# All four queues written in another order between the output projection and the third normalisation of a decoder layer

## The reference

```python
x = x + attn(_layernorm(x), Wqkv, bqkv, Wo, bo)            # one head, 256 wide
x = x + xattn(_layernorm(x), ctx_4096, scales, zero_points)
x = x + ffn(_layernorm(x), c1_w, c2_w, w1, w2t)

def xattn(x1, x2, ...):
    fake_quant(x, s, z) = (clip(round(x / s + z), 0, 255) - z) * s
    return matmul(fake_quant(x1), fake_quant(x2))           # (512x1024) @ (1024x1024) per batch

def ffn(xf, c1_w, c2_w, w1, w2t):
    inter = xf @ c1_w.T @ c2_w.T                            # rank 16, 3584 wide
    idx = argmax of every block of 64 in inter              # one of 64 hidden units is kept
    h = relu(sum(w1[idx] * xf)); return h @ w2t[idx]
```

## Time and profile before

| | before |
|---|---|
| median of 3 runs | 806.68 us (805.74 to 808.58) |
| the profiled execution | 806.61 us, of which 804.8 us are the span of the trace |
| busy: PE, DVE, POOL, ACT | 787.0, 591.8, 432.8, 248.8 us |
| mean granted clock of TensorE | 0.997 of full speed |

### The profile page before, as it was taken

One profiled execution on the slowest core, in us unless ns is written; L12 is line 12 of the kernel. 1 busy time (PEld: TensorE's weight loads), 2 busy tenths in 40 slices (PEclk: granted clock), 3 DMA queues, 4 the chain that ended last, 5 costly groups with the idle time before them and its releaser, 6 DMA issues.

```text
span 804.8 us, 11466 instructions
## 1 busy us (share of the span) xinstructions
PE 787.0 (98%) x3884; PEld 640.1 (80%) x3888; DVE 591.8 (74%) x958; ACT 248.8 (31%) x372; POOL 432.8 (54%) x264
## 2 busy tenths in 40 slices
PE   8999998799999999999999999999999999999998
PEld 7888886358888888888888888888888888888886
DVE  6646648768786778777787878787878777787864
ACT  6456655775141121222212030303121212212030
POOL 3936797556999974352525344444444452525340
PEclk9999999999999999999999999999999999999999
DMA  9126403000101111111111110111111111111104
GB/s 344 56 105 208 157 1 109 0 8 7 40 24 50 59 53 60 53 59 52 59 52 59 52 47 19 49 54 52 59 52 59 52 59 52 59 52 52 52 11 198
DMA packets 22615, 53.22 MB, mean 66 GB/s; under 512 B 4544, under 2 KB 6592, under 8 KB 22464
## 3 DMA queue, kind: packets, MB, share of 16 engines
q1 hardware_dynamic: 22448, 51.86, 18.7%
q10 hardware_dynamic: 144, 1.05, 0.4%
HBM read 48.70 MB, written 4.19 MB: 66 GB/s over the span
## 4 chain that ended last, share of the span: by engine, by line
PE 89%; DVE 6%; ACT 3%; POOL 1%; DMA 1%; issue 1%; DVEq 0%; ACTq 0%
PE bank L1747 13%; PE bank L1748 13%; PE bank L1749 13%; PE bank L1652 12%; PE bank L1654 11%; PE bank L1653 11%; PE bank L1463 3%; PE bank L1465 3%; PE bank L1464 3%; PE bank L1661 2%; PE bank L1643 2%; PE bank L1606 1%; DVE xn L1127 1%; PE bank L1622 1%; DVE stats L1012 1%
## 5 line engine op out<-in xcount | busy, mean ns | idle before, releaser
L1747 PE MATMUL bank<-w_hi,h_hi 128*128 128x512 f32 x448 | 176.2, 393 | 0.0
L1748 PE MATMUL bank<-w_lo,h_hi 128*128 128x512 f32 x448 | 175.0, 391 | 0.0
L1749 PE MATMUL bank<-w_hi,h_lo 128*128 128x512 f32 x448 | 174.4, 389 | 0.0
L1249 DVE TENSOR_TENSOR x<-bank,x 128x512 f32<-128x512 f32 x208 | 133.4, 685 | 50.0 <-PE bank L1749 50.0
L559 POOL TENSOR_TENSOR lo_r<-r,slot 128x512 fp32r<-128x512 f32 x52 | 67.5, 1299 | 163.7 <-ACT slot L777 163.7
L1749 PEld LDWEIGHTS bank<-w_hi,h_lo 128*128 128x128 f32 x448 | 84.1, 188 | 18.0
L1747 PEld LDWEIGHTS bank<-w_hi,h_hi 128*128 128x128 f32 x448 | 84.1, 188 | 15.7
L1748 PEld LDWEIGHTS bank<-w_lo,h_hi 128*128 128x128 f32 x448 | 84.4, 188 | 15.2
L1652 PE MATMUL bank<-xT_hi,slot 128*128 128x512 f32 x240 | 95.0, 396 | 0.0
L1653 PE MATMUL bank<-xT_lo,slot 128*128 128x512 f32 x240 | 93.6, 390 | 0.0
L1654 PE MATMUL bank<-xT_hi,lo_r 128*128 128x512 f32 x192 | 74.8, 390 | 0.0
(11 more groups left out here) (203 smaller groups left out, 1598.3 us busy)
## 6 DMA issues: line engine op xcount, KB each, us to landing
r<-w SPq DMA_DIRECT2D x56, 256.0 KB, 3.4
w_raw<-w SPq DMA_DIRECT2D x28, 512.0 KB, 4.0
x<-x_in SPq DMA_DIRECT2D x8, 512.0 KB, 9.7
ctx_raw<-ctx_in SPq DMA_DIRECT2D x8, 512.0 KB, 3.9
xn<-ctx_in SPq DMA_DIRECT2D x8, 512.0 KB, 4.8
out<-x SPq DMA_DIRECT2D x7, 512.0 KB, 2.7
W_raw<-wqkv SPq DMA_DIRECT2D x6, 512.0 KB, 9.8
c_raw<-c SPq DMA_DIRECT2D x112, 16.0 KB, 2.0
```

The costliest lines, as they stand in the source:

```text
L1249: nc.vector.tensor_tensor(x[:, t, c], bank[unit_banks(g)[p]][:, :], x[:, t, c], ALU.add).then_inc(unit_added, 1)
L1747: nc.tensor.matmul(dst, h_hi[:, j, m], w2_hi[:, j, c], start=j == 0, stop=False)
L1748: nc.tensor.matmul(dst, h_hi[:, j, m], w2_lo[:, j, c], start=False, stop=False)
L1749: last = nc.tensor.matmul(dst, h_lo[:, j, m], w2_hi[:, j, c], start=False, stop=j == GJ - 1)
```

## The change

The same instructions are issued but for two PE placements that were "halfway" inside a product; their order in the queues of PE, DVE, ACT and POOL is another, and the job list with it. SP's queue is unchanged. In the order of PE: all four Wo products of the first batch come first, then the first column sums, then both O halves with nothing between them and Wo 4. Quantised products 0 and 1 stand between Wo products 5, 6 and 7. Third-norm transposes are spread between the quantised products, and those of tiles 6 and 7 come behind C11.

```diff
@@ job_order
-    jobs += both("WO", 0) + both("WO", 1) + both("WO", 2) + both("O", 1) + both("WO", 3) + both("CB", 0)
-    jobs += both("WO", 4) + both("WO", 5) + both("CB", 1) + both("WO", 6) + both("WO", 7)
...
+    for t in range(4):
+        jobs += both("WO", t)
+    jobs += both("CB", 0) + both("O", 1) + both("WO", 4) + both("WO", 5) + both("XA", 0) + both("WO", 6) + both("WO", 7)
+    jobs += both("XA", 1) + both("CB", 1) + both("XA", 2) + both("XA", 3) + both("XA", 4) + both("XA", 5)
+    jobs += both("T3", 0) + both("T3", 1) + both("XA", 6) + both("T3", 2) + both("T3", 3) + both("XA", 7)
+    jobs += both("T3", 4) + both("T3", 5)
     jobs += [("U", 0)] + both("T3", 6) + both("T3", 7)
@@ gpsimd
-            for t in range(6):
+            add_corr(0)
+            add_corr(1)
+            add_corr(2)
+            plain_lo(0, 0)
+            for t in range(3, NT):
+                add_corr(t)
...
+            for t in range(4):
                 norm3(t)
-            plain_lo(0, 0)
             plain_lo(0, 1)
-            norm3(6)
-            norm3(7)
+            for t in range(4, NT):
+                norm3(t)
@@ scalar
             variance(2, 3)
             roots(2, 0)
-            copy_q1T(7)
             variance(2, 4)
+            centre_q1(6)
+            centre_q1(7)
+            copy_q1T(6)
+            both(hi_T, 2, 0)
+            both(hi_T, 2, 1)
...
+            plain_hi(0, 2)
+            plain_hi(0, 3)
             both(hi_T, 2, 6)
             both(hi_T, 2, 7)
-            plain_hi(0, 2)
-            plain_hi(0, 3)
             hi_w2(0, 0)
@@ vector
+            for t in range(TB):
+                add_WO(t)
             copy_CB(0)
             norm_scale(1, 0)
+            lo_O(1, 0)
+            round_q1(0)
+            lo_O(1, 1)
+            round_q1(1)
             add_WO(4)
...
+            add_XA(3)
+            add_XA(4)
+            norm_scale(2, 0)
+            round_q1(6)
+            round_q1(7)
+            add_XA(5)
             row_biases()
...
             lo_u(0)
             cut_c2(0)
+            dve.wait_ge(order_ready, 1)
+            pick_first(0, 0)
             lo_T(2, 6)
             lo_T(2, 7)
@@ tensor
+            for t in range(TB):
+                project_out(t)
+            column_sums(0)
             mix_values(1, 0)
             mix_values(1, 1)
-            project_out(3)
-            column_sums(0)
             project_out(4)
-            project_out(5)
-            column_sums(1)
-            project_out(6)
             pe.wait_ge(id_b_ready, 1)
             transpose_q1(0)
+            project_out(5)
+            transpose_q1(1)
+            quantised_product(0)
+            project_out(6)
+            transpose_q1(2)
             project_out(7)
-            transpose_q1(1)
-            for t in range(6):
-                quantised_product(t, lambda: transpose_q1(t + 2))
-            quantised_product(6)
+            quantised_product(1)
+            transpose_q1(3)
+            column_sums(1)
+            quantised_product(2)
+            transpose_q1(4)
+            quantised_product(3)
+            transpose_q1(5)
+            quantised_product(4)
+            quantised_product(5)
+            transpose_q1(6)
             transpose_norm(2, 0)
             transpose_norm(2, 1)
+            quantised_product(6)
+            transpose_q1(7)
+            transpose_norm(2, 2)
+            transpose_norm(2, 3)
             quantised_product(7)
-            for t in range(2, 6):
-                transpose_norm(2, t)
+            transpose_norm(2, 4)
+            transpose_norm(2, 5)
             rank_projection(0)
-            transpose_norm(2, 6)
-            transpose_norm(2, 7)
...
             plain_hidden(0, 0, 0, within({4: [(score_pair, 0)]}))
+            transpose_norm(2, 6)
+            transpose_norm(2, 7)
             plain_hidden(0, 1, 0, within({1: [(score_pair, 1)]}))
```

More of the change, by code:

```diff
@@ L549, in norm3 @@
                                         ALU.add).then_inc(normed3, 1)
[L551 to L554, removed]
             def lo_A(g, i, raw, hi, lo):
@@ L894, in _ @@
             nc.scalar.activation(eps_root, eps, ACT.Sqrt)
-            variance(1, 0)
-            variance(1, 1)
-            variance(1, 2)
+            for t in range(TB):
+                variance(1, t)
+            roots(1, 0)
             hi_O(1, 0)
+            norm(1, 0)
             hi_O(1, 1)
-            variance(1, 3)
-            roots(1, 0)
-            norm(1, 0)
             norm(1, 1)
             centre_q1(0)
+            centre_q1(1)
             norm(1, 2)
-            centre_q1(1)
             copy_q1T(0)
             norm(1, 3)
+            plain_hi(0, 0)
             centre_q1(2)
+            centre_q1(3)
             copy_q1T(1)
-            centre_q1(3)
             roots(1, 4)
             copy_q1T(2)
+            variance(2, 0)
             norm(1, 4)
@@ L918, in _ @@
             copy_q1T(3)
+            centre_q1(5)
+            variance(2, 1)
+            copy_q1T(4)
             roots(1, 6)
-            centre_q1(5)
+            variance(2, 2)
             norm(1, 6)
-            variance(2, 0)
-            copy_q1T(4)
+            copy_q1T(5)
             norm(1, 7)
[L925 to L930, removed]
             variance(2, 3)
             roots(2, 0)
-            copy_q1T(7)
             variance(2, 4)
+            centre_q1(6)
[3 more added lines that the diff above has]
+            both(hi_T, 2, 1)
             variance(2, 5)
             roots(2, 4)
-            both(hi_T, 2, 0)
-            both(hi_T, 2, 1)
-            plain_hi(0, 0)
             plain_hi(0, 1)
-            variance(2, 6)
+            copy_q1T(7)
             both(hi_T, 2, 2)
             both(hi_T, 2, 3)
+            variance(2, 6)
+            both(hi_T, 2, 4)
+            both(hi_T, 2, 5)
             variance(2, 7)
             roots(2, 6)
-            both(hi_T, 2, 4)
-            both(hi_T, 2, 5)
             hi_u(0)
+            plain_hi(0, 2)
+            plain_hi(0, 3)
             both(hi_T, 2, 6)
             both(hi_T, 2, 7)
-            plain_hi(0, 2)
-            plain_hi(0, 3)
             hi_w2(0, 0)
@@ L1593, in transpose_q1, with quantised_product @@
                 last.then_inc(q1T_done, 1)
-            def quantised_product(t, halfway=lambda: None):
+            def quantised_product(t):
                 pe.wait_ge(q1T_copied, t + 1)
@@ L1601, in quantised_product @@
                 for n in range(2):
-                    if n == 1:
-                        halfway()
                     take_bank("XA", t, n)
```

53 lines of the change are left out of this document (16 added, 37 removed).

## The result

| | before | after |
|---|---|---|
| median, us | 806.51 (805.62 to 808.58, 13 runs) | 803.88 (802.84 to 805.26, 13 runs) |
| ratio, 95% interval | 1 | 0.9967 [0.9959, 0.9976] |
| the profiled execution, us | 806.61, span 804.8 | 803.34, span 801.5 |
| first Wo matmul to first mask of group 0, us | 204.62 - 106.09 = 98.53 | 201.35 - 106.64 = 94.71 |

A forecast was written before the change was run, and what follows sets the result against it. TensorE was taken as the bound, with 13.6 us lost beyond its work from Wo 0 to U. Less 5.3 us of new waits, the gain was 8.3, put at 8.2, giving 798.4 us (range 795.9 to 801.9).

The forecast's parts named there:

- The work and the loss of before: From Wo 0 to the end of U, 81.7 us: 68.1 priced as TensorE work, 13.6 as lost.
- step (d): Score pair 0 in the middle of C11 waits for cut_c2, held up by GpSimd; priced 1.9 us (0.3 to 2.2).
- The waits on the q1 copy go: TensorE's three waits for ScalarE's copy before quantised-input transposes, 6.9 us in all, were to vanish.
- Step (a): Wo 4 waits for the low part of the second O half, no longer hidden by Wo 3; priced 1.7 us.
- Step (b): The transpose of q1 tile 6, right behind XA 5, waits for its queued rounding and centring; priced 1.3 us.
- Step (c): Third-norm transposes of tiles 0 and 1 wait for GpSimd's norm3, held up by two roundings; priced 0.4 us.
- Rival 2: More lost than walked through, from thin handovers or a clock fall of 1.7 us; 801.4 us, chance 0.18.
- Rival 1: cut_c2 and norm3 don't meet, so Step (c) and step (d) shrink to 0.3; 796.4 us, chance 0.14.
- Rival 3: Nothing gained: the VectorE and ScalarE ring bounds the stretch and waits move elsewhere; 805 to 807 us, chance 0.05.
- Rival 4: Slower: GpSimd's sums become the bound at the first looped group; 811.6 us, chance 0.03.

The follow-up runs named there:

- e5: Changed kernel with GpSimd's last context-sum addition behind its first zero-point addition, and cut_c2(0) ahead of the third norm's last scale; 797.96 us.
- e2: Changed kernel with GpSimd's last context-sum addition moved behind its first zero-point addition, VectorE's queue unchanged; 801.47 us.
- e3: Changed kernel with cut_c2(0) moved ahead of the third norm's last scale on VectorE; 800.34 us.
- e6: e5 with Wo 4 beginning on the first O half in both banks, and tile 6's rounding and centring moved earlier; 797.24 us.
- e8: Changed kernel with its last part undone: transposes of third-norm tiles 6 and 7 ahead of C11 again; 803.08 us.
- e1: Changed kernel with two VectorE lines swapped: the cut of the second O half ahead of the rounding of tile 0; 802.28 us.
- e4: Changed kernel with the edits of e1 and e3 together: O cut ahead of the rounding, cut_c2 early; 799.09 us.
- e9: e5 with transposes of third-norm tiles 6 and 7 put back ahead of C11; 799.97 us.

## Why the prediction was wrong in size

- **The work and the loss of before (68.1 and 13.6 us).** Nearly right, as far as e5 tests it. The stretch forecast for after was 98.53 - 8.2 = 90.3 us; e5 has nothing of step (d), priced 1.9, so by the same sum it would take 88.4, and it took 88.91. The rest, 0.5, is about the 0.6 that stays spread between 127 and 180 us.
- **The waits on the q1 copy go.** Right: none is left.
- **Step (a), Wo 4, priced 1.7, measured 3.4.** This is the step that failed first. It let the rounding of tile 0 cost what it costs beside a resting GpSimd (0.69, from rows at 158 us) and gave the queue position 0.1 to 0.2. GpSimd was summing the context in that place, in before too (its six additions run to 125.2 there), and the prediction had this very mechanism in hand for steps (c) and (d). In before the rounding came at 128.75, after the sums had ended; the change brought it forward into them. e2 shows that it was this. The trace of before had a warning, a rounding beside GpSimd's additions (timeline of VectorE, before):

```profile
134.70 2.71 DVE L1127 TENSOR_SCALAR xn<-xn 128x1024 f32<-128x1024 f32 x1
```

- **Step (b), priced 1.3, measured 1.15 to 1.2.** Right. **Step (c), priced 0.4:** the next product started 1.97 us after the sixteen transposes did, where two such tiles took 1.67 in the earlier trace rows: 0.3. Right, and by the mechanism given: VectorE's two roundings went first (161.47), and GpSimd's four norm3 behind them took 5.61 us where they took 4.74 in before.
- **Step (d), priced 1.9, measured 2.4.** Mechanism right, place right, size 0.5 too small. The walk had norm3 on GpSimd from 0.4 to 2.8 us after U, holding the CAST, and one weight cut, holding the second operation. But norm3 began 0.16 us before the end of U, so the first weight cut began at 182.68, 0.10 us before the CAST, and held it (1.34 instead of 0.29), and a second weight cut held the second operation. The "Who interferes with whom" section of "SBUF — State Buffer" in the Trainium skill says that whoever issues first has the shared pair for the whole instruction and the other blocks fully. The rows of after agree three times over (the held instruction ended 0.2 to 0.5 us after GpSimd's); it was the right rule to weigh, applied in one place too few.
- **Rival 2** (more lost, with a fall of the clock of 1.7 us, 801.4) is nearest to what came. It was given 0.18, with the argument that no new wait would be over 1.9 us. With (a) and (d) at 3.25 and 2.23 that argument was gone. This is the second step that failed, and the largest term of the miss: a new fall was put at nothing. The clock cost after 2.6 us a run where it had cost before 1.9; the forecast counted 1.7 of it as regained and none as new.
- **Rival 1** (the meeting on cut_c2 doesn't happen) didn't come about; e3, where it was made not to happen, gives its price: 2.5 us in the stretch. **Rival 3** is refuted by e5. **Rival 4** didn't come: no wait of TensorE at the first looped group. The timelines of GpSimd (three rows) and TensorE, of after:

```profile
193.98 4.77 POOL L558 TENSOR_TENSOR w_lo<-w_raw,w_hi 128x1024 fp32r<-128x1024 f32 x2 [8.75 <-ACT w_hi L794]
198.71 2.39 POOL L569 TENSOR_TENSOR T_raw<-xT_hi,xT_hi 128x1024 f32<-128x1024 f32 x1
...
285.22 1.29 POOL L553 TENSOR_TENSOR cut_tmp<-tmp,slot 128x512 fp32r<-128x512 f32 x1 [0.16 <-POOL r L642]
...
287.97 0.39 PE L1647 MATMUL bank<-T_hi,slot 128*128 128x512 f32 x1
```

  The w2 cuts waited 8.75 us for ScalarE, and the sums started at 198.71 and not near 194, later even than the 198.41 of the earlier trace rows. Still the cut for the group ended at 286.51 and TensorE is at its place in the earlier trace rows at 287.97: 1.46 us of slack, where 1.3 had been forecast. That the two agree is in part luck: both ends came 4.7 to 4.9 us later than the walk had them (281.8 and 283.05). In e6, with 9.3 us won in its profile, it is 1.34.

For the whole time, about: 5.5 us short of the forecast = 1.7 (a) + 0.5 (d) + 2.4 (clock: 2.6 in the mean of 13 runs, where the forecast left 1.9 - 1.7 = 0.2) + 0.9 not located, of which 0.6 is the spread between 127 and 180 us. What the profile doesn't settle is which wait brings the clock down. The same wait before Wo 4 (3.21 to 3.25 us) was followed by a fall in e3 and e8 and by none in after; the same 2.23 before the score pair came with one in after and e2 and with none in e1. And e3 and e8, whose only wait over 1.2 us is the one before Wo 4, lost 1.6 and 2.9 us a run. So it is shown that kernels with waits of 2.2 us and more lost to the clock and those without hardly did, but not what decides in one execution.

## What to carry to other kernels

When an instruction is moved, look at what the *other* engines do at its new time, not at its old one: VectorE's SBUF-only instructions (rounding, cast, two-operand cuts) cost here 0.3 to 0.7 us beside a resting GpSimd and up to 2.7 beside a working one, and everything queued behind them pays. Put such instructions where GpSimd waits (e3), or give GpSimd its rest where they are (e2), before changing VectorE's own order, which in e1 moved 1.1 of 1.8 us one step on. And an edit may look bad only because it took another one's cover away: the tail cost 1 to 1.8 us until cut_c2 was moved, and then was worth 2.2.

## What the runs showed of the hardware

- In these rows VectorE and GpSimd don't share, one stands still until the other's instruction has ended: the rounding of a 128x1024 tile took 0.69 us with GpSimd idle (e2, 123.78) and 2.39 beside an addition of GpSimd (after, 123.87). Two in a row took 1.29 where they were first (after, 161.47), and up to 4.98 between GpSimd's additions (e6).
- GpSimd pays too. Its context additions took 2.2 us each in a row of their own (13.27 for six in after, 11.08 for five in e2), but the one that e2 moved in among the roundings took 2.60 (126.68). Its zero-point additions took 4.67 for two with no rounding beside them (after, 149.78) and 5.64 with one (after, 125.68).
- A pair of dependent VectorE instructions loses twice: GpSimd's next instruction began between the two halves of cut_c2 (its second weight cut at 183.92, the first half ending at 184.12), so each half waited for one weight cut. The prediction had counted one weight cut for both.
- The granted clock halved near the end of a wait of 2.2 to 3.5 us, from 0.1 us before it (e2) to 1.2 us behind it (after), not every time, while TensorE was busy from then on; it cost 1.6 to 1.7 us each time. Kernels without such waits vary less, though not all of them: the four runs of e5 lie within 0.11 us and those of e6 within 0.31, but those of e4 within 1.2 and of e9 within 1.5, the thirteen of after within 2.4.
